# Forget gate first, half of a table on GpSimd, taps moved by sixteen DMAs, film products and low lags spread through the selection

## The chip, the cores and the metric

The kernel runs on one core of a Trainium2 chip, as one program written by hand: each engine has its own list of instructions, and the lists are held together by semaphores alone. PE is the matmul engine (TensorE), DVE the vector engine, ACT the scalar engine, POOL is GpSimd, and SP only issues transfers. The metric is the time in microseconds (us) of one execution on the device, the median of several runs. Lower is better.

## The reference, cut to what matters

A two-layer decoder: x is 2 x 512 rows of 128 numbers, the context 2 x 154 rows of 96, all float32. The first layer is a gated recurrence over a batch of two, a cross-attention with FiLM and an S4D convolution, and attention with experts; the second has two attentions and experts again. The change touches only the first two parts of layer 0:

```python
feat = x @ W_in
V, Q, Fg = jnp.split(feat, 3, axis=-1)
V = gelu(V); Q = gelu(Q); Fg = sigmoid(Fg)
...                                        # a recurrence over the batch axis (2 steps)
x = _layernorm(x + o @ W_out)

scores = einsum('bthd,bghd->bhtg', x @ Wq, ctx @ Wk) / sqrt(32)      # 4 heads, 154 keys
topv, topi = top_k(scores, 32); probs = softmax(topv)
attn_mean = scatter(probs).mean(heads); c_t = attn_mean @ (ctx @ Wv)
y = layernorm(x) * (1 + gate * scale_in(c_t)) + gate * shift_in(c_t)
dtA = exp(log_dt)[:, None] * (A_re + 1j * A_im)                      # 128 channels, 64 states
dC = C * (exp(dtA) - 1) / A
K = 2 * real(einsum('dn,dnl->dl', dC, exp(dtA[:, :, None] * arange(512))))
y = irfft(rfft(y, 1024) * rfft(K, 1024))[:512] + y * D_skip
```

## The kernel before

The 1024 rows are eight tiles (t = 0 to 7) of 128. Everything lies in SBUF; there are eight PSUM banks of 512 columns.

**First stage** (`a_pe`, `a_act`, `a_dve`). PE multiplies the three thirds of `W_in` (values, queries, forget gate, in this order), ACT makes gelu, gelu and sigmoid of them, DVE combines them (`keys`, `qk`, `carried`, `mixed`), PE multiplies `W_out`, DVE adds and normalises in two halves (`norm`, L188 the last step of it; the root is POOL's, L244). Ahead of `keys` DVE computes the table of the convolution (`b_dve_stack`, L419 to L460): eight blocks of 64 columns in `stack`, which PE transposes and ACT copies (`b_act_stack_in`, L528).

**Convolution taps**. The 512 lags are split into 32 low and 16 high ones. `low_r`, `high_r` get angles (ACT, L468 and L475: one instruction for each lag), DVE takes the whole turns off (`b_dve_rounds`: L482 for all 4096 low columns, L484 for the 2048 high ones), POOL subtracts (L494 twice for the low halves, L489 for the high one), ACT takes absolute value and sines (L547, L549, L550, L556) and, later, exponentials (`b_act_low_rates` L534 in two runs of 16 lags, `b_act_high_rates` L541). POOL multiplies: high factors 0 to 3 (L502 twice, L504, L507) and the low factors (L516 twice, by halves of the columns). Then `taps_of_lags` (L735) is 128 small matmuls, one for each channel, 4 to a group of 32 rows of bank 3. ACT copies bank 3 into `taps` by sixteen instructions of 32 rows each, since the row group changes (`b_act_taps`, L566); POOL adds the skip line (L1052), and `taps_spectrum` (L804) transforms `taps`.

**Selection** (`b_dve_attention`). For 16 pairs j of tile and head, DVE finds the 32 largest of 154 scores (`peak` L850, `select` L865 to L877, `selected` L886, `shares` L893, L897). Each pair needs ACT's `exponentials(j)` (L930, L931), which need the peaks, which need the scores (PE L724, copied by `scores_in` L920). PE `gather(t)` (L748, L752) transposes and adds the heads once `diagonals(t)` (L944) are there, ACT copies (`attn_in` L1017, L1018), PE `film_tile(t)` (L790, L791), ACT `film_in(t)` (L952), POOL `modulate(t)` (L1038, L1039), PE `spectrum(t)` (L775). The orders in `b_act_attention`, `b_pool_attention` and `b_pe_attention` are written out by hand, and each engine keeps to its own. After spectrum(7) come DVE products (L1153 on) and the inverse transform on PE (L1092).

Before the selection POOL scales the FiLM weights (`b_pool_pre`, L668 to L672), makes the masks, takes the roots, marks attention columns with a memset (L690), and between the angles and the factors writes the FiLM rows (`b_pool_film_rows`, L654 to L660).

## Time and profile before

| | us |
|---|---|
| median of 3 runs (663.29 to 664.49) | 663.56 |
| the profiled execution | 663.11 |
| its span in the trace | 661.3 |
| PE busy (share of the span) | 603.2 (91%) |
| DVE busy | 439.0 (66%) |
| ACT busy | 287.9 (44%) |
| POOL busy | 246.5 (37%) |

The profiled execution is 0.45 us under the median; 1.8 us of it lie outside the span. The first 130 us hold all that the change touches. The shares of the whole span say little about them: there PE waits longest, and afterwards it is nearly always busy. "Granted clock" is TensorE's clock as a share of full speed: 1.00 and 0.50 are its two levels, 2.4 and 1.2 GHz. Records that overlap in the trace are pipelined.

### The profile page before, as it was taken

What the parts mean: (1) busy time and instruction counts of PE and PEld (TensorE: products, weight loads), DVE (VectorE), ACT (ScalarE), POOL (GpSimd) and SP (SyncE); (2) the same over time, 40 slices, a digit from 0 to 9 for tenths busy, and PEclk for the clock granted to TensorE, in tenths of its full rate; (3) what the DMA queues carried; (4) which work ended last, traced back from release to release, by engine and by line L of the source; (5) the groups of instructions that cost most, each with busy time, mean ns of one, the idle gap of its engine ahead of it and who ended that gap; (6) DMA issues with size and microseconds to landing.
All of it is one profiled execution on the core that took longest, in us unless ns stands there. A gap on an engine that the chain in (4) does not pass through costs nothing.

```text
span 661.3 us, 8811 instructions
## 1 busy us (share of the span) xinstructions
PE 603.2 (91%) x3171; PEld 302.0 (46%) x3172; DVE 439.0 (66%) x1173; ACT 287.9 (44%) x548; POOL 246.5 (37%) x179
## 2 busy tenths in 40 slices
PE   8864959998997999999999998999977999999997
PEld 4432548886572332222222442233622345556566
DVE  6899998556559846766776569668645675333335
ACT  7979968213230554444444333534232334221210
POOL 2899271422531344655465344557334100000001
PEclk9955879999999899999999999999979999999999
DMA  8300006021000000000000000000600000000001
GB/s 321 110 0 0 2 1 256 1 68 60 1 0 1 0 0 1 0 1 1 0 1 0 1 1 0 1 0 1 268 22 1 0 1 0 1 1 0 1 0 33
DMA packets 4945, 19.25 MB, mean 29 GB/s; under 512 B 2053, under 2 KB 3462, under 8 KB 4390
## 3 DMA queue, kind: packets, MB, share of 16 engines
q1 hardware_dynamic: 4902, 18.69, 7.5%
q8 instruction: 25, 0.41, 0.3%
q14 instruction: 18, 0.15, 0.1%
HBM read 18.16 MB, written 0.52 MB: 28 GB/s over the span
## 4 chain that ended last, share of the span: by engine, by line
PE 71%; DVE 14%; ACT 7%; POOL 4%; issue 4%; DMA 0%; POOLq 0%; DVEq 0%; ACTq 0%
PE PS L2401 11%; PE PS L1606 9%; PE PS L1622 8%; PE PS L2422 6%; PE PS L1564 5%; PE PS L1590 3%; PE PS L1692 2%; PE PS L1636 2%; PE PS L1609 2%; DVE SB L1853 2%; DVE SB L199 2%; PE PS L2091 2%; POOL SB L238 2%; ACT SB L468 1%; DVE SB L212 1%
## 5 line engine op out<-in xcount | busy, mean ns | idle before, releaser
L1853 DVE TENSOR_REDUCE SB<-PS 128x2 f32<-128x1024 f32 x64 | 78.4, 1226 | 62.9 <-PE PS L1590 62.8
L1839 POOL TENSOR_TENSOR SB<-SB 128x1024 f32<-128x1024 f32 x32 | 75.2, 2352 | 108.7 <-ACT SB L1791 107.8
L1791 ACT ACTIVATE SB<-PS 128x1024 f32<-128x1024 f32 x64 | 65.6, 1024 | 102.3 <-PE PS L1609 102.2
L2401 PE MATMUL PS<-SB 128*128 128x512 f32 x176 | 78.4, 594 | 0.0
L1606 PE MATMUL PS<-SB 64*128 64x512 f32 x256 | 70.4, 627 | 1.1 <-ACT SB L1795 1.1
L1622 PE MATMUL PS<-SB 128*64 128x512 f32 x256 | 67.6, 610 | 0.5 <-DVE SB L1885 0.5
L238 POOL TENSOR_TENSOR SB<-SB 128x4 f32<-128x4 f32 x18 | 19.3, 1073 | 116.9 <-DVE SB L204 104.3
L2460 ACT ACTIVATE SB<-PS 128x512 f32<-128x512 f32 x44 | 26.2, 597 | 80.2 <-PE PS L2401 78.8
L2486 DVE TENSOR_TENSOR SB<-SB,PS 128x512 f32<-128x512 f32 x44 | 30.0, 688 | 41.8 <-PE PS L2401 40.5
L1876 DVE RECIPROCAL SB<-PS 128x256 f32<-128x256 f32 x32 | 55.6, 1744 | 0.0
L2401 PEld LDWEIGHTS PS<-SB 128*128 128x128 f32 x176 | 32.2, 190 | 35.3 <-issue 33.7
L2466 POOL TENSOR_TENSOR SB<-SB 128x4 f32<-128x4 f32 (+2 forms) x3 | 2.6, 861 | 115.3 <-DVE SB L2510 115.3
L2422 PE MATMUL PS<-SB 128*128 128x128 f32 x320 | 40.0, 280 | 0.0
L1843 POOL TENSOR_TENSOR SB<-SB 128x1024 f32<-128x1024 f32 x16 | 38.2, 2386 | 1.3
L1564 PE MATMUL PS<-SB 128*128 128x512 f32 x64 | 37.4, 667 | 0.7 <-ACT SB L1774 0.7
L2422 PEld LDWEIGHTS PS<-SB 128*128 128x128 f32 x320 | 36.9, 192 | 1.9
L1606 PEld LDWEIGHTS PS<-SB 64*128 64x128 f32 x256 | 20.8, 186 | 29.7 <-issue 13.0
L1622 PEld LDWEIGHTS PS<-SB 128*64 128x64 f32 x256 | 14.3, 135 | 32.7 <-issue 23.8
L1783 ACT ACTIVATE SB<-PS 128x512 bf16<-128x512 f32 x32 | 19.1, 597 | 22.1 <-PE PS L1564 20.9
L2498 DVE SCALAR_TENSOR_TENSOR SB<-PS,SB 128x128 f32<-128x128 f32 x32 | 11.2, 351 | 25.6 <-PE PS L2422 25.5
L1590 PE MATMUL PS<-SB 64*128 64x512 bf16 x128 | 24.7, 382 | 3.2 <-DVE SB L1853 3.2
L869 DVE MAX8 SB<-SB 128x8 f32<-128x154 f32 x96 | 25.6, 308 | 0.0
(415 smaller groups left out, 1125.2 us busy)
## 6 DMA issues: line engine op xcount, KB each, us to landing
SB<-exp SPq DMA_DIRECT2D x1, 4352.0 KB, 14.1
SB<-moe SPq DMA_DIRECT2D x1, 4096.0 KB, 14.5
SB<-dft SPq DMA_DIRECT2D x1, 2304.0 KB, 11.6
SB<-att SPq DMA_DIRECT2D x1, 2048.0 KB, 8.2
SB<-mix SPq DMA_DIRECT2D x1, 768.5 KB, 4.4
SB<-mix SPq DMA_DIRECT2D x1, 640.0 KB, 5.5
SB<-ssm SPq DMA_DIRECT2D x1, 602.0 KB, 6.6
SB<-lat SPq DMA_DIRECT2D x1, 585.0 KB
```

Source lines behind the costliest of these rows:

```text
L238: pool.tensor_tensor(rstd[:, a:z], variance[:, a:z], minus_half[:, a:z], ALU.pow).then_inc(sem("norm_rstd"), 1)
L1564: pe.matmul(bank(b), w[:, 128 * pair:128 * pair + 128], xsT[:, 512 * batch:512 * batch + 512], start=True, stop=True)\
L1590: ins = pe.matmul(bank(4 + h), qb_ring[i % 3][head(h), 128 * qt:128 * qt + 128], kb_ring[i % 3][head(h), :], start=True, stop=True)
L1606: pe.matmul(bank(2 * (n % 2) + h), k_ring[i % 3][head(h), 128 * u:128 * u + 128], q_ring[i % 3][head(h), :], start=True, stop=False)
L1622: ins = pe.matmul(heads_bank(i)[head(h), :], v, expd[i % 2][:, 1024 * kt + 512 * h:1024 * kt + 512 * h + 512], start=(kt == 0), stop=(kt = ...
L1791: act.activation(expd[i % 2][:, 1024 * u:1024 * u + 1024], bank(2 * (u % 2), 2), ACT.Exp).then_inc(sem("d_exp"), 1)
L1839: pool.tensor_tensor(half_sums[half], e[:, 0:1024], e[:, 1024:], ALU.add).then_inc(sem("d_half_sum"), 1)
L1843: pool.tensor_tensor(key_sum, half_sums[0], half_sums[1], ALU.add).then_inc(sem("d_key_sum"), 1)
L1853: dve.tensor_reduce(shift[i % 2][:, qt:qt + DK + 1:DK], two_heads(bank(4, 2)), AX_X, ALU.max, negate=True)\
L1876: ins = dve.reciprocal(unit[:, 256 * k:256 * k + 256], bank(7)[:, 256 * k:256 * k + 256])
L2401: pe.matmul(bank(2 * (i % 3) + side), w, xsT[:, 512 * n:512 * n + 512], start=True, stop=True).then_inc(sem(("top2_w1", "top2_w3")[side]), 1)
L2422: ins = pe.matmul(banks[k][:, 0:128], hidden[q][:, h:h + 128], exp_w["e_w2"][:, at:at + 128], start=False, stop=(c == WHOLE - 1))
```

## The change

1. **First stage**: PE multiplies the forget third first, then queries, then values; ACT makes the sigmoid first. DVE forms `keys` and `carried` as soon as the forget gate is there, `qk` after the queries. The keys and values of the context go to banks 4 and 5, their wait stands before `W_out`, and the score weights (`b_pe_scorer`) follow both halves of `W_out`. The normalisation is unrolled (statistics of half 1 ahead of the last step of half 0).
2. **Table**: DVE keeps the first four blocks of `stack` and the reciprocal. The other seventeen multiplies, adds and three negations are on POOL (`b_pool_stack`). PE transposes two blocks early and two late; DVE copies the first two, ACT the others. DVE makes 8 of the 32 low-lag angles (L470 of the new file), ACT 24.
3. **Rounds by pieces**: low half 0, peak(0), low half 1, peak(1), and the high ones after select(1). The memset of the marked columns moves from POOL to DVE.
4. **POOL's order**: the FiLM weights come after the roots, then both low angles, the marks, the FiLM rows, then the high angles. Low factors go by halves of the lags (strided) with modulate in between; modulate(2) now stands before high factor 3.
5. **ACT's order**: xsT's second half and 14 of the high angles move into the selection; the absolute value stands before exponentials(5), the sines after scores_in(4).
6. **PE's order**: the second half's transposes after score(0), the FiLM products after score(1), spectrum(2) ahead of `taps_of_lags`, spectrum(4) and (5) earlier.
7. **Taps**: one ACT copy into `staged`, then sixteen DMAs of 32 x 128 numbers on SP (`b_sp_taps`), ahead of the transfer of the `moe` weights.

```diff
@@ a_pe
-        for m in range(3):
+        for i in range(2):
+            ins = pe.transpose(bank(7)[:, 128 * i:128 * i + 128], stack[:, 128 * i:128 * i + 128], ident)
+        ins.then_inc(sem("s_stack_turned"), 1)
+        for m in (2, 1, 0):
@@ a_dve
-        dve.wait_ge(sem("a_gates"), 3)
+        dve.wait_ge(sem("a_gates"), 1)
         follow(dve.tensor_scalar(keys, forget, one_less, None, ALU.mult))
+        follow(dve.scalar_tensor_tensor(carried[:, 0:512], keys[:, 512:], 1.0, keys[:, 0:512], ALU.subtract, ALU.mult))
+        dve.wait_ge(sem("a_gates"), 2)
...
+        add(0)
+        spread(0)
+        variances(0)
+        add(1)
+        spread(1)
+        norm_apply(dve, tiled(xsum), tiled(xs), 0).then_inc(sem("stage_half"), 1)
+        variances(1)
+        norm_apply(dve, tiled(xsum), tiled(xs), 1).then_inc(sem("stage_done"), 1)
@@ rounds and angles
-    def b_dve_rounds(dve):
+    def b_dve_low_rounds(dve, h):
+        c = slice(2048 * h, 2048 * h + 2048)
         dve.wait_ge(sem("s_low_products"), 1)
-        dve.tensor_scalar(low_k, low_r, MAGIC, MAGIC, ALU.add, ALU.subtract).then_inc(sem("s_rounds"), 1)
+        dve.tensor_scalar(low_k[:, c], low_r[:, c], MAGIC, MAGIC, ALU.add, ALU.subtract).then_inc(sem("s_rounds"), 1)
+    def b_dve_high_rounds(dve):
         dve.wait_ge(sem("s_high_turns"), 1)
@@ b_pool_high_angles
-        pool.wait_ge(sem("s_rounds"), 2)
+        pool.wait_ge(sem("s_rounds"), 3)
@@ b_pool_low_factor
-        c = slice(2048 * h, 2048 * h + 2048)
-        pool.wait_ge(sem("s_rates"), 1)
-        pool.wait_ge(sem("s_low_waves"), h + 1)
+        lags = slice(LOW // 2 * h, LOW // 2 * h + LOW // 2)
+        pool.wait_ge(sem("s_rates"), h + 1)
+        pool.wait_ge(sem("s_low_waves"), 2)
@@ taps
-        for q in range(a, z):
-            for j in range(4):
-                act.activation(to[32 * q:32 * q + 32, :, :, j], tp[32 * j:32 * j + 32, :, :, q], ACT.Copy)\
-                   .then_inc(sem("s_taps_copied"), 1)
+        act.activation(staged.rearrange("p (q c g) -> p g c q", q=4, c=4), bank(3).rearrange("p (g c q) -> p g c q", c=4, q=4),
+                       ACT.Copy).then_inc(sem("s_taps_copied"), 1)
+    def b_sp_taps(sp):
+        sp.wait_ge(sem("s_taps_copied"), 1)
+        for j in range(4):
+            for q in range(4):
+                sp.dma_start(taps[32 * q:32 * q + 32, 128 * j:128 * j + 128], staged[32 * j:32 * j + 32, 128 * q:128 * q + 128])\
+                  .then_inc(sem("s_taps_copied"), 16)
@@ b_dve_attention
-        b_dve_rounds(dve)
+        b_dve_low_rounds(dve, 0)
         dve.wait_ge(sem("masks_in"), 1)
         peak(0)
+        b_dve_low_rounds(dve, 1)
         peak(1)
+        dve.memset(attn1[96:128, :], 1.0).then_inc(sem("x_clear"), 1)
...
+            if j == 1:
+                b_dve_high_rounds(dve)
@@ b_pool_attention
-        pool.wait_ge(sem("s_taps_copied"), 16)
+        pool.wait_ge(sem("s_taps_copied"), 257)
```

The places on which most rests are these. **POOL**, from the last step of its preparation to the absolute value's input. Before (L668 to L672 are the FiLM weights, L244 the roots, L494 the low and L489 the high angles, L654 to L660 the FiLM rows):

```order
L681 MEMSET SB 1x128 [waits pool_step]
L244 TENSOR_TENSOR SB<-SB 128x4 [waits norm_variance,masks_in]
L244 TENSOR_TENSOR SB<-SB 128x4 [waits norm_variance]
L686 TENSOR_SCALAR SB<-SB 1x128 [waits norm_rstd]
L687 CAST SB<-SB 128x8 [waits pool_step]
L688 TENSOR_SCALAR SB<-SB 128x8 [waits pool_step]
L690 MEMSET SB 32x1024 [waits a_features,pool_step]
L494 TENSOR_TENSOR SB<-SB 128x2048 [waits s_rounds,x_clear]
L489 TENSOR_TENSOR SB<-SB 128x2048 [waits s_rounds]
L494 TENSOR_TENSOR SB<-SB 128x2048 [waits s_rounds]
L654 TENSOR_SCALAR SB<-SB 32x512 [waits s_low_products]
```

And in the change (L238 the roots, L739 to L743 the FiLM weights, L540 the low angles, L714 to L720 the FiLM rows, L535 the high angles):

```order
L238 TENSOR_TENSOR SB<-SB 128x4 [waits norm_variance]
L739 TENSOR_SCALAR SB<-SB 128x512 [waits ssm_in]
L741 TENSOR_TENSOR SB<-SB 128x128 [waits film_w_in]
L742 TENSOR_TENSOR SB<-SB 128x128 [waits pool_step]
L743 TENSOR_TENSOR SB<-SB 128x128
L540 TENSOR_TENSOR SB<-SB 128x2048 [waits s_rounds,film_w_in]
L540 TENSOR_TENSOR SB<-SB 128x2048 [waits s_rounds]
L748 TENSOR_SCALAR SB<-SB 1x128 [waits norm_rstd]
L749 CAST SB<-SB 128x8 [waits pool_step]
L750 TENSOR_SCALAR SB<-SB 128x8 [waits pool_step]
L714 TENSOR_SCALAR SB<-SB 32x512 [waits masks_in]
```

and, without a gap, the rest of the FiLM rows, the high angles and what reads them:

```order
L715 TENSOR_SCALAR SB<-SB 32x2x128 [waits pool_step]
L716 TENSOR_TENSOR SB<-SB 32x128 [waits pool_step]
L717 TENSOR_TENSOR SB<-SB 32x128 [waits pool_step]
L718 TENSOR_TENSOR SB<-SB 32x128 [waits pool_step]
L720 COPY SB<-SB 32x512 [waits pool_step]
L720 COPY SB<-SB 32x512 [waits film_w_in]
L535 TENSOR_TENSOR SB<-SB 128x2048 [waits s_rounds,film_w_in]
L1100 TENSOR_TENSOR SB<-SB 128x8 [waits s_high_turns]
```

The memset is gone; the FiLM weights, a second low half and the FiLM rows now stand ahead of the high angles.

**SP**, the transfer queue, in the change (the line before and the two behind the new ones are as they were, under other numbers):

```order
L1301 DMA SB<-mha 128x1164 [waits film_w_in,x_inputs]
L619 DMA SB<-SB 32x128 [waits s_taps_copied]
L619 DMA SB<-SB 32x128 x15
L1303 DMA SB<-moe 128x8192
L1305 DMA SB<-att 128x4096 [waits s_conv]
```

Sixteen transfers are added, and the `moe` weights go behind them.

**PE** around `taps_of_lags` (L795 in the change; L835 a spectrum, L808 and L812 a gather, L850 and L851 a film tile, L864 the transform of the taps):

```order
L835 MATMUL PS<-SB 128x128 x8
L795 MATMUL PS<-SB 32x16 x128
L808 MATMUL PS<-SB 128x128 x4
L812 MATMUL PS<-SB 32x128 x3
L812 MATMUL PS<-SB 26x128
L835 MATMUL PS<-SB 128x128 x8
L850 MATMUL PS<-SB 128x512
L851 MATMUL PS<-SB 128x512
L864 MATMUL PS<-SB 128x128 x16
```

The first row, spectrum(2), stood behind the second before; what is left between the taps and their transform is one gather, one spectrum and one film tile.

## Rows read from the trace of the kernel before

**Rows 1.** The chain of work that ended last, in time: start us, us, what.

```profile
79.95 9.07 POOL SB L516 x2
89.01 4.47 POOL SB L507
93.61 2.85 PE PS L735 x197
...
...
98.69 3.03 PE PS L775 x16
101.73 0.89 PE PS L748 x8
...
106.67 3.57 PE PS L804 x32
```

**Rows 2.** Timeline, PE: the last gather and the last spectra.

```profile
118.53 1.05 PE L748 MATMUL PS<-SB 128*128 128x128 f32 x8
...
124.00 5.52 PE L775 MATMUL PS<-SB 128*128 128x128 f32 x48
```

**Rows 3.** Timeline, POOL, 24 to 49 us.

```profile
24.14 1.04 POOL L244 TENSOR_TENSOR SB<-SB 128x4 f32<-128x4 f32 x1 [1.00 <-DVE SB L182]
...
29.59 5.45 POOL L494 TENSOR_TENSOR SB<-SB 128x2048 f32<-128x2048 f32 x1
35.00 4.53 POOL L489 TENSOR_TENSOR SB<-SB 128x2048 f32<-128x2048 f32 x1
...
44.12 0.70 POOL L654 TENSOR_SCALAR SB<-SB 32x512 f32<-32x512 f32 x1
...
48.72 0.20 POOL L1030 TENSOR_TENSOR SB<-SB 128x8 f32<-128x8 f32 x1
```

**Rows 4.** Groups of POOL to 125 us: busy us, mean ns, idle before.

```profile
L1063 POOL TENSOR_TENSOR SB<-SB 128x512 f32<-128x512 f32 x1 | 1.3, 1276 | 0.0
L1038 POOL TENSOR_TENSOR SB<-SB 128x128 f32<-128x128 f32 x7 | 2.9, 414 | 17.6 <-ACT SB L952 17.5
```

**Rows 5.** Timeline, DVE and POOL side by side.

```profile
29.43 1.23 DVE L484 TENSOR_SCALAR SB<-SB 128x2048 f32<-128x2048 f32 x1 [0.81 <-ACT SB L475]
141.18 1.08 POOL L1068 TENSOR_TENSOR SB<-SB 128x512 f32<-128x512 f32 x1
141.24 1.87 DVE L212 TENSOR_SCALAR SB<-SB 128x128 f32<-128x128 f32 x4 [1.13 <-POOL SB L238]
162.07 1.12 DVE L212 TENSOR_SCALAR SB<-SB 128x128 f32<-128x128 f32 x4 [1.12 <-POOL SB L238]
```

**Rows 6.** Timeline, ACT, 45 to 85 us.

```profile
45.28 1.90 ACT L547 ACTIVATE SB<-SB 128x2048 f32<-128x2048 f32 x1
...
84.21 0.62 ACT L952 ACTIVATE SB<-PS 128x512 f32<-128x512 f32 x1
```

**Rows 7.** Timeline: ACT's copies of the taps, and SP's issue of small transfers.

```profile
98.73 6.67 ACT L566 ACTIVATE SB<-PS 32x128 f32<-32x128 f32 x16 [3.62 <-PE PS L735]
5.53 0.32 SPq L286 DMA_DIRECT2D SB<-lines  x1
481.62 1.17 SPq L1949 DMA_DIRECT2D SB<-exp  x2
```

**Rows 8.** DMA issues: KB each, median us from issue to landing.

```profile
SB<-exp SPq DMA_DIRECT2D x2, 32.0 KB, 2.1
```

**Rows 9.** Windows of PE: us, length, busy (records), granted clock.

```profile
88.00:89.00 1.00, 0.44 (x9) 1.00 0.00 0
90.00:91.00 1.00, 0.00 (x0) 0.81 0.00 0
...
100.00:101.00 1.00, 1.00 (x7) 0.57 0.51 164
```

**Rows 10.** Timeline, DVE: the selection's longest wait and its last instruction.

```profile
106.15 0.09 DVE L865 MATCH_VALUE_LOAD SB<-SB 128x8 f32 x1 [2.83 <-ACT SB L931]
...
114.79 0.17 DVE L897 RECIPROCAL SB<-SB 128x4 f32<-128x4 f32 x1
```

More of the change, by code:

```diff
@@ L326, in a_pe @@
             ins.then_inc(sem("a_out"), 1)
-            if half == 0:
-                b_pe_scorer(pe)
+        b_pe_scorer(pe)
+        pe.wait_ge(sem("s_stack"), 1)
+        pe.wait_ge(sem("s_stack_in"), 1)
+        for i in (2, 3):
+            ins = pe.transpose(bank(7)[:, 128 * i:128 * i + 128], stack[:, 128 * i:128 * i + 128], ident)
+        ins.then_inc(sem("s_stack_turned"), 1)
     def a_act(act):
@@ L336, in a_act @@
         act.wait_ge(sem("a_features"), 6)
-        act.activation(forget, bank(4, 2), ACT.Sigmoid, scale=-1.0).then_inc(sem("a_gates"), 1)
+        act.activation(gate_v, bank(0, 2), ACT.Gelu).then_inc(sem("a_gates"), 1)
     def a_dve(dve, follow):
@@ new lines, in b_dve_stack, with b_pool_stack @@
+        dve.tensor_copy(stack_T[:, 0:256], bank(7)[:, 0:256]).then_inc(sem("s_stack_in"), 1)
+        dve.wait_ge(sem("s_stack_in"), 1)
+        for l in range(LOW_ACT, LOW):
+            ins = dve.tensor_scalar(lag(low_r, LOW)[:, :, l], turn_T, float(l), ssm["quarter"], ALU.mult, ALU.add)
+        follow(ins)
+    def b_pool_stack(pool, follow):
+        tt = lambda o, a, b, op: pool.tensor_tensor(o, a, b, op)
+        s = stack.rearrange("p (k n) -> p k n", n=N_ST)
+        pool.wait_ge(sem("table_in"), 16)
+        pool.wait_ge(sem("s_trig"), 2)
@@ L665, in b_pool_pre @@
         pool.memset(rest_V, 0.0).then_inc(sem("x_clear"), 1)
+        b_pool_stack(pool, follow)
         pool.wait_ge(sem("small_in"), SMALL)
+        follow(pool.tensor_copy(mask_line, ctx_bytes))
+        follow(pool.tensor_scalar(mask_line, mask_line, 1.0, -NEG, ALU.subtract, ALU.mult))
+        by_batch = mask_line.rearrange("p (b g) -> p b g", b=B)
+        m2 = mask_low.rearrange("p (b h g) -> p b h g", b=B, h=2)
+        for h in range(2):
+            pool.tensor_copy(m2[:, :, h, :], by_batch)
+        pool_rstd_half(pool, 0)
+        pool.tensor_copy(ones_low, ones[0:1, :])
+        pool.memset(zeros_low, 0.0).then_inc(sem("masks_in"), 1)
+        pool_rstd_half(pool, 1)
         pool.wait_ge(sem("ssm_in"), 16)
@@ L805, in taps_spectrum @@
                                     mat[:, 512 * c + 128 * j:512 * c + 128 * j + 128],
-                                    taps[:, 128 * c:128 * c + 128], start=(c == 0), stop=(c == 3))
+                                    taps_of[:, c], start=(c == 0), stop=(c == 3))
             ins.then_inc(sem("s_taps_dft"), 1)
-        for t in range(4):
+        score(0)
+        b_pe_turn(pe, 1)
+        score(1)
+        b_pe_film(pe)
+        for t in (2, 3, 4):
             score(t)
-        score(4)
         gather(0)
@@ L832, in b_pe_attention @@
         gather(6)
+        spectrum(4)
         film_tile(5)
@@ L836, in b_pe_attention @@
         gather(7)
-        spectrum(4)
+        spectrum(5)
         film_tile(7)
-        for t in (5, 6, 7):
+        for t in (6, 7):
             spectrum(t)
@@ L964, in b_act_attention @@
         exponentials(4)
+        b_act_high_sizes(act)
+        exponentials(5)
+        scores_in(4)
         b_act_high_waves(act)
@@ L972, in b_act_attention @@
         exponentials(7)
-        scores_in(4)
         film_in(0)
@@ L1044, in b_pool_attention @@
         modulate(0)
+        b_pool_low_factor(pool, 0)
         modulate(1)
[L1046 removed]
         b_pool_low_factor(pool, 1)
+        modulate(2)
         b_pool_high_factor(pool, follow, 3)
[L1049 removed]
         modulate(3)
[L1051 to L1052 removed]
+        pool.wait_ge(sem("s_taps_copied"), 257)
+        first = taps_of[0:1, 0]
+        pool.tensor_tensor(first, first, skip_line.rearrange("p (j g) -> p j g", j=4), ALU.add).then_inc(sem("s_taps_in"), 1)
         modulate(4)
```

184 lines of the change are left out of this document (92 added, 92 removed).

## The prediction

> **What bounds the kernel now.** I read the chain of waits in time first, since shares of the span say nothing of 130 us in which every engine waits in turn. From 93.61 us it is PE alone: the channel matmuls of the taps (L735) until 98.69, then spectra, gathers and film tiles, the transform of the taps at 106.67, and the last spectrum, whose record ends at 129.5 [rows 1, 2]. So what counts is when PE gets its taps and whether it ever waits behind them. Ahead of 93.61 the chain is POOL: two low factors from 79.95 (9.07 us, waiting for ACT's exponentials) and high factor 3 to 93.5 [rows 1]. ACT itself works through a fixed list from the absolute value at 45.28 to the third film copy at 84.21 [rows 6]; nearly all of it is back to back. The selection on DVE is long, but what ends last is not DVE: it is done at 114.9, and the last gather starts at 118.5 [rows 2, 10]. Its one long wait, 2.83 us, is for ACT, which is then busy with sixteen copies of the taps (6.67 us) [rows 7, 10].
>
> I call S the start of the absolute value on ACT, A the end of high factor 3, T the last channel matmul, X the start of the taps' transform. Now S = 45.3, A = 93.5, T = 98.7, X = 106.7, end of spectra 129.5.
>
> **The first stage.** The forget gate first lets DVE start `keys` when its own table is done. Without the table's second half that is near 10 us, when before it waited for the third of three activations to near 13; and the root of the first stage comes about 1 us before the 25.2 us of now [rows 3] (the rest of the gain goes to PE, whose three pair sums are then late, and to the unrolled halves). On POOL the seventeen moved operations of 64 columns, at most 0.41 us each, the mean of 128 columns [rows 4], fill time in which POOL waited for transfers. I cost all of this at nothing but the 1 us: its cover is that nothing waits for DVE's selection by itself: DVE could be 3.6 us later before the last gather is [rows 2, 10], and more in the change, where X is later. A high round of 1.23 us [rows 5] and the memset go into the selection, and use up what the earlier start gives.
>
> **S, the term I trust least.** ACT is ready for the absolute value at about 45 as before. But it needs the high angles, and these now stand last in POOL's list. Before, POOL had done them at 39.5 (35.00 plus 4.53), with one low angle and the FiLM rows still to come [rows 3]. Now, from the second root at 24.2: FiLM weights 2.6 (1.28 for 512 columns, three of 0.41 [rows 4], and gaps), two low angles 9.1, marks 1.2, FiLM rows 4.6 (44.12 to 48.72), high angles 4.5 [rows 3]. That sums to 46.2. This is the lower bound.
>
> To it comes what DVE does to POOL. Three rows show the engines holding each other up: beside a POOL operation of 1.08 us that had begun 0.06 us before them, four normalising operations of DVE took 1.87 us, elsewhere 1.12; and POOL's first low angle took 5.45 us, the next operation of the same size 4.53, where DVE's high rounds ran beside the first [rows 3, 5]. In the change DVE does its second four normalising operations (1.1 us), two low rounds and a high one (1.23 each) [rows 5] while POOL is in this list without a pause. Each costs POOL its length if it has to wait, nothing if both can go on: 0 to 4.8 us. I take 4.1, near the upper end, since both rows show a wait of nearly the whole overlap. S = 50.3, 5.0 later than now.
> The Trainium skill (SBUF — State Buffer, "SBUF: two separate sides") says that whichever of GpSimd's operation and a two-port or two-input DVE operation starts first holds the shared ports for its whole length, and the other stands still. By it the sum is S = 50.3 as taken, and DVE's rounds may also be held up by up to a whole 4.5 us operation; if ports were shared by bandwidth S would be 46 to 48. The two rows agree with the rule, as far as pairs that short can.
>
> **A.** ACT's list from S to the end of film copy 2 holds the same work as now (exponentials(5) and scores_in(4) only move within it), 38.9 us to that copy's start and 0.6 for it [rows 6]. I add 1.0 for gather(2) and score(6), which PE, idle longer, still does at half clock. So film copy 2 is there at 90.8. New is that modulate(2) (0.9, two of 0.41 [rows 4]) and then high factor 3 (4.5) stand behind it: A = 96.2. The low factors no longer bind: the second gets its exponentials 5 us before that copy and takes 4.5 [rows 1]. Its strided form is not in the trace; between the broadcast high factors and twice the plain one, it is 3.7 to 9 us, and only above 5.5 would it count. A is 2.7 later than now, though S is 5.0 later, since low factor 2 now runs beside ACT's high exponentials. The lower bound from S = 46.2 is 92.1.
>
> **T.** Before, PE stood idle from 88.4, its clock fell after about 2.4 us of that and was back only at 100.9 [rows 9], so the channel matmuls ran at half clock and took 5.1 us with a pause of 1.2 us in them [rows 1]. With spectrum(2) moved into that gap no idle time above 2 us is left, and they run at full clock: 3.9, between 3.1 (all halved but the pause) and 5.1. T = 100.1, which is 1.4 later than now.
>
> **X.** Now 7.9 us lie between T and X, all PE's own work. In the change spectrum(2) is gone from there, and 4.9 are left (101.73 to 106.67 [rows 1]). The taps' way in the change is: one ACT copy 0.6, as film copies of the same size take [rows 6]; SP's start 0.1; sixteen issues; 2.1 from the last issue to its landing [rows 8]; POOL's skip line 0.45; gaps 0.2. A small transfer of 32 rows took SP 0.32, with its gap 0.36, and of 64 rows 0.58 [rows 7]; SBUF to SBUF is not in the trace. Fifteen issues ahead of the last are thus 5.4 to 8.7; I take 5.7, since 32 rows it is. Sum 9.1: X = 109.2, and PE waits 4.2 us. That ACT's copies fall from 6.67 to 0.6 us frees the selection (its 2.83 us wait) but not PE. The range is T plus 8.8 to T plus 12.1. The `moe` weights are issued 6 us later, with 40 us until their use.
>
> **The clock behind X.** 4.2 us without work are more than the 2.4 us after which the clock fell before, and it then took PE 7.3 us from its restart (93.6) to be back [rows 9]. At half clock 7.3 us do the work of 3.65; I take 3.2 lost, 0 if it stays up, 3.65 at most. From X on the same matmuls are left as now, 22.8 us at full clock. The end of spectra is 109.2 + 22.8 + 3.2 = 135.2, against 129.5: 5.7 later. Behind it nothing changes, and PE waits for those spectra before the inverse, so all of it counts. 663.1 + 5.7 = **668.8 us** against the profiled execution; the median of before is 0.45 higher, and I leave that difference in the range.
>
> **Rivals.** (1) *The clock holds* through the 4.2 us: 668.8 - 3.2 = 665.6. For it: the wait is not much longer than 2.4 us. Against: that row.
> (2) *Faster: POOL is not held up and the clock holds.* With S = 46.2, A = 92.1 and X = 105.1, end 127.9, 1.6 earlier: 661.5. The point from which it decides is S = 47.8 with the clock up; with the clock down S would have to be 44.6, below what ACT allows. For it: POOL's waits for DVE are seen for one or two operations only, and the first stage may bring the roots more than 1 us forward. Against: the rows named.
> (3) *The parts cancel*: S near 48 and no loss of clock, or S at 46 with a short one: 662.5 to 664.5.
> (4) *Later still*: SP needs 0.55 for each transfer (X 2.8 later), and DVE's rounds wait for whole POOL operations and POOL for them (S 2 later): 673.6. The selection might then bind too. For it: 0.58 for 64 rows. Against: 0.32 for 32.
> (5) *The change doesn't do what it says*, since ACT, not POOL, sets S: that needs POOL's list of 22 us to fit into 21, rival 2 in effect.
>
> **How the numbers follow.** Forecast 0.50 (own range 666.3 to 671.5, from S 48 to 52.4 and the bounds of T), rival 1 0.17, rivals 2 and 5 0.14, rival 3 0.10, rival 4 0.09. The range 662.0 to 672.5 leaves out half of rival 2 and most of rival 4 and the forecast's tails, 2 in 10. A measurement of this kernel can tell about 0.2% (1.3 us) from no change. Slower by more: the forecast, rival 1 and rival 4 less a few tails, 0.71; within: rival 3 and tails, 0.14; faster: 0.15.
>
> **What would show it.** In the changed profile: the high angles of POOL (L535) end near 50 and the absolute value (L591) starts right behind them; exponentials(6) keep DVE waiting about 2 us near 64; high factor 3 (L553) ends near 96; no half clock at the channel matmuls (L795); one ACT copy of the taps and sixteen issues of about 0.36; PE's longest wait, about 4 us, right ahead of L864, ended by POOL's skip line, and half clock for some 7 us behind it. If L535 ends before 47, or the wait ahead of L864 is under 2 us, the forecast falls; if ACT's list is much shorter than 39 us, too.

## The result and the profile after

The kernel after took 673.88 us (median of four runs, 670.33 to 675.15), beside 663.61 us for the kernel before: ratio 1.0137, 95% interval 1.0101 to 1.0172. Seven further runs on other occasions, six of them against 23 of before, gave 667.98 to 673.96: ratio 1.0094, interval 1.0062 to 1.0127. A ratio is estimated from all runs of both kernels except those more than 1.5% above the fastest run of their kernel, and is not the quotient of the two medians (1.0155 here). The kernel is slower, as forecast. The first median lies above the forecast range, and the profiled run (670.33, span 668.5) inside it, 1.5 us above the forecast. What lies behind each is taken apart below.

The timeline of PE in the kernel after shows the stretch at issue (start us, us, engine line, operation, count, in brackets the idle time ahead and what ended it):

```profile
93.67 1.69 PE L795 MATMUL PS<-SB 128*32 128x16 f32 x181
97.36 0.82 PE L795 MATMUL PS<-SB 128*32 128x16 f32 x75 [1.99 <-issue]
...
103.84 1.02 PE L851 MATMUL PS<-SB 128*128 128x512 f32 x2
111.30 5.97 PE L864 MATMUL PS<-SB 128*128 128x128 f32 x32 [6.44 <-POOL SB L1123]
...
132.82 3.73 PE L835 MATMUL PS<-SB 128*128 128x128 f32 x32
136.74 0.49 PE L1163 MATMUL PS<-SB 128*128 128x128 f32 x2 [0.19 <-DVE SB L1248]
```

A spectrum (L835, from 91.56) now stands ahead of the channel matmuls (L795), and T, the end of their last, is at 98.2, where it was 98.7 [rows 1]. Then PE has 6.7 us of work left and stands still for 6.44 us, until POOL's skip line (L1123) releases the transform of the taps (L864) at X = 111.3, in place of 106.7 [rows 1]. That transform takes 5.97 us, where the same 32 matmuls took 3.73 at full clock in the kernel before. The inverse (L1163) starts at 136.74, where it started at 129.71: 7.0 us later. The profiled runs differ by 7.2 (668.5 against 661.3 us of span). What follows is unchanged: from that point to the first matmul of the last stage it is 403.3 us in this trace and 403.1 in that of before.

What PE waits for is told by the timelines of ACT, SP and POOL, and by the list of DMA issues (KB each, median us from issue to landing):

```profile
98.23 1.07 ACT L611 ACTIVATE SB<-PS 128x512 f32<-128x512 f32 x1 [1.45 <-PE PS L795]
...
99.33 10.10 SPq L619 DMA_DIRECT2D SB<-SB  x16
...
110.71 0.45 POOL L1123 TENSOR_TENSOR SB<-SB 1x128 f32<-1x128 f32 x1 [15.79 <-DMA SB<-SB]
```

```profile
SB<-SB SPq DMA_DIRECT2D x16, 16.0 KB, 1.8
```

The whole way of the taps can be added up: copy 1.07 (to 99.30), sixteen issues in 10.1 us, the last of them begun at 108.8, about 1.9 from there until POOL, released by its landing, starts the skip line (110.7), the skip line 0.45, and X at 111.3. An issue takes 0.59 us (shortest 586 ns, longest 604), 0.63 with the gap to the next. That is the largest piece, and the DMA engines are not what it waits for: they are busy 11% of the time from 100 to 110 us.

Ahead of it POOL's list and ACT show what became of S and A:

```profile
23.23 1.57 POOL L739 TENSOR_SCALAR SB<-SB 128x512 f32<-128x512 f32 x1
24.89 1.51 POOL L741 TENSOR_TENSOR SB<-SB 128x128 f32<-128x128 f32 x1
...
26.89 1.44 POOL L743 TENSOR_TENSOR SB<-SB 128x128 f32<-128x128 f32 x1
28.40 9.05 POOL L540 TENSOR_TENSOR SB<-SB 128x2048 f32<-128x2048 f32 x2
...
38.60 0.70 POOL L714 TENSOR_SCALAR SB<-SB 32x512 f32<-32x512 f32 x1
39.39 1.72 POOL L715 TENSOR_SCALAR SB<-SB 32x256 f32<-32x256 f32 x1
...
44.05 4.51 POOL L535 TENSOR_TENSOR SB<-SB 128x2048 f32<-128x2048 f32 x1
...
83.15 4.67 POOL L563 TENSOR_TENSOR SB<-SB 128x2048 f32<-128x2048 f32 x1 [3.56 <-ACT SB L580]
...
88.98 4.55 POOL L553 TENSOR_TENSOR SB<-SB 128x2048 f32<-128x2048 f32 x1
```

The high angles (L535) end at 48.56, and ACT's absolute value starts at once, S = 48.6. High factor 3 (L553) ends at A = 93.5, where it ended before.

### The profile page after: what moved, and what is told of

Same layout as the page of the kernel before. It is cut to its first block, busy times and chain, and to the rows that moved or that the text cites. A ratio compares the mean times of both kernels' runs of the same rounds, so it can differ in the third digit from the quotient of the medians.

```text
span 668.5 us, 8816 instructions
## 1 busy us (share of the span) xinstructions
PE 601.2 (90%) x3170; PEld 301.4 (45%) x3170; DVE 438.8 (66%) x1164; ACT 279.7 (42%) x525; POOL 251.9 (38%) x198
## 4 chain that ended last, share of the span: by engine, by line
PE 70%; DVE 18%; ACT 6%; issue 3%; POOL 2%; SPq 1%; DMA 0%; POOLq 0%; DVEq 0%; ACTq 0%
PE PS L2472 11%; PE PS L1677 8%; PE PS L1693 8%; PE PS L2493 5%; PE PS L1635 4%; PE PS L1661 3%; PE PS L1707 2%; DVE SB L212 2%; POOL SB L238 2%; DVE SB L199 2%; PE PS L1680 2%; DVE SB L1924 2%; PE PS L2162 2%; PE PS L864 1%; SPq L619 1%
## 5 line engine op out<-in xcount | busy, mean ns | idle before, releaser
L2472 PE MATMUL PS<-SB 128*128 128x512 f32 x176 | 78.4, 594 | 0.0
L238 POOL TENSOR_TENSOR SB<-SB 128x4 f32<-128x4 f32 x20 | 21.3, 1068 | 119.5 <-DVE SB L204 103.6
L2557 DVE TENSOR_TENSOR SB<-SB,PS 128x512 f32<-128x512 f32 x44 | 30.0, 687 | 41.8 <-PE PS L2472 40.5
L1635 PE MATMUL PS<-SB 128*128 128x512 f32 x64 | 36.7, 657 | 0.7 <-ACT SB L1845 0.7
L850 PE MATMUL PS<-SB 128*128 128x512 f32 x16 | 9.5, 679 | 18.7 <-ACT SB L1089 18.1
```

The costliest lines, as they stand in the source:

```text
L238: pool.tensor_tensor(rstd[:, a:z], variance[:, a:z], minus_half[:, a:z], ALU.pow).then_inc(sem("norm_rstd"), 1)
L1635: pe.matmul(bank(b), w[:, 128 * pair:128 * pair + 128], xsT[:, 512 * batch:512 * batch + 512], start=True, stop=True)\
L2472: pe.matmul(bank(2 * (i % 3) + side), w, xsT[:, 512 * n:512 * n + 512], start=True, stop=True).then_inc(sem(("top2_w1", "top2_w3")[side]), 1)
```

## The experiments

**Theory A** was: X is late because of the sixteen transfers, 0.63 us each on one queue, and the copy ahead of them; nearly all of the 7 us is this. **Rivals**: POOL's longer list (S and A late) or the rest of the rearrangement costs it; or the half clock behind the wait is the larger part.

**The taps moved by ACT again.** Only the mover goes back; the channel order and the new layout stay.

```diff
-        act.activation(staged..., bank(3)..., ACT.Copy)          # one copy, then sixteen DMAs on SP
+        for q in range(4):
+            for j in range(4):
+                act.activation(to[32 * q:32 * q + 32, j], tp[32 * j:32 * j + 32, :, :, q], ACT.Copy)
```

> The kernel after, but the taps go to their places by ScalarE's sixteen copies, as in the kernel before, into the new layout; no transfers. Theory A (the sixteen transfers at 0.63 us each set the start X of the taps' transform): X comes about 8 us behind the last channel matmul instead of 13.1, at 106.2, TensorE waits 1.4 us there instead of 6.4, and if the clock then holds another 2.4 us are saved: 663 to 666 us. Theory B (what is late is not the mover but GpSimd's longer list before it, and the rest of the stage): the time stays within 2 us of the kernel after, 670 to 675 us, and the wait on GpSimd ahead of the transform is still 4 us or more.

The profiled run took 661.48 us, nine others 659.96 to 666.55 (median of all 665.42, that of before on this occasion 663.36; ratio to before 1.0007, interval 0.998 to 1.0033). PE, ACT and POOL in its trace:

```profile
97.68 0.82 PE L799 MATMUL PS<-SB 128*32 128x16 f32 x75 [2.19 <-issue]
...
98.55 4.70 ACT L615 ACTIVATE SB<-PS 32x128 f32<-32x128 f32 x16 [1.65 <-PE PS L799]
...
103.33 0.45 POOL L1127 TENSOR_TENSOR SB<-SB 1x128 f32<-1x128 f32 x1 [8.29 <-ACT SB L615]
...
103.93 3.81 PE L868 MATMUL PS<-SB 128*128 128x128 f32 x32 [0.28 <-POOL SB L1127]
...
127.71 1.16 PE L1167 MATMUL PS<-SB 128*128 128x128 f32 x8 [0.19 <-DVE SB L1252]
```

X comes 5.4 us behind T, not 8 as expected, PE waits 0.28 us in place of 6.44, the clock stays full, and the inverse starts at 127.7: 9.0 us before that of the kernel after, and 2.0 before that of the kernel before. Theory A stands, and the rival that puts the cost into the rest of the change falls: without the transfers the rest gains 2 us in this trace. The runs as a whole do not show that gain: the interval of the ratio includes 1. The part on the spread of the runs looks at why single traces and medians differ. A part of the 9.0 us need not be the mover's. In after the clock was also at half from 99 to 102 us, right behind the pause of 1.99 us in the channel matmuls; there it cost nothing, since PE had to wait anyway. In this trace it did not fall there, though the pause was 2.19 us. With the 6.7 us of work that PE had behind T in after, X would have been at 105.2 here, 1.3 us later than it was. The sixteen copies are shorter than I had them: 4.70 us, where the kernel before needed 6.67 [rows 7]. One takes 270 ns (median of sixteen) in place of 394. The operation, its size and its source are the same; what differs is where it writes, 128 adjacent elements per row of the new layout where the old one wrote every fourth. By this sum the new layout shortens the copies by 2.0 us, which is all that the trace gains over before; the old layout was not run with the rest of the change. The change gave the layout to a mover that did not show this gain.

**The other way round: the transfers put into the kernel before.** It is the same mover with its channel order and layout, without anything else of the change.

```diff
-        b_act_taps(act, 0, 4)
+        b_act_taps(act)            # one copy into `staged`
@@ c_sp
-        sp.wait_ge(sem("s_taps"), 1)
+        b_sp_taps(sp)              # sixteen transfers, ahead of the experts' weights
```

> The kernel BEFORE with one part of the change alone: the taps moved by one ScalarE copy and sixteen transfers on SP, with the channel order that goes with them. Theory A (the mover is what costs): the transform of the taps starts 13.1 us behind the last channel matmul instead of 8.0, at 111.8 instead of 106.7, TensorE waits about 5 us, and with the half clock behind that wait the end of the spectra moves by 5 to 7.5 us: 668.5 to 671 us, as slow as the whole change. Theory B (the mover costs only in the company of the rest): under 666 us.

670.32 us (668.68 to 670.89; ratio 1.0083, interval 1.0059 to 1.0107). In its trace:

```profile
98.11 1.04 PE L742 MATMUL PS<-SB 128*32 128x16 f32 x59 [1.40 <-issue]
...
112.25 5.44 PE L811 MATMUL PS<-SB 128*128 128x128 f32 x32 [4.40 <-POOL SB L1060]
...
137.16 1.16 PE L1100 MATMUL PS<-SB 128*128 128x128 f32 x8 [0.19 <-DVE SB L1185]
```

X is 13.1 us behind T (99.15), as in the kernel after, the sixteen issues take 10.09 us, and the inverse starts at 137.16, 7.5 us later than before. So the mover alone costs all that the change costs. Taken away it gives 9, put in alone it takes 7.5. One reason can be read off: here a spectrum still stands behind the channel matmuls, and PE waits 4.40 us where it waited 6.44.

**The clock.** Twenty-four idle matmuls (their result is never read) fill the larger part of PE's wait ahead of the transform: 5.5 us of work, and 3.29 without.

```diff
                 pe.wait_ge(sem("x_scores_in"), NT)
+                stay_warm(pe, 24, 1, ident)
                 pe.wait_ge(sem("s_taps_in"), 1)
```

> The kernel after with 24 idle matmuls on TensorE (their result is never read) ahead of its wait for the taps, so that it does not stand still for 6.4 us there; the wait itself stays. If the half clock behind the wait is the wait's doing, the first transform of the taps takes 3.7 us instead of 6.0 and X stays at 111.3: 2.4 us faster than the profiled run of after, 668 us, and the runs draw together. If the clock falls for what came earlier (the stall in front of the channel matmuls), nothing changes: 670 to 675 us.

The profiled run took 669.38 us, the five others 668.11 to 673.3; the median is 672.5, the ratio to before 1.0134 (interval 1.0099 to 1.0169). On the same occasion the kernel after had a median of 670.28, so the runs as a whole gained nothing, and what follows rests on the traces. Here is PE's granted clock (third number from the end) in two stretches of after, and then one of this kernel:

```profile
106.00:108.00 2.00, 0.00 (x0) 0.00 (x0) 2.00 (x13) 1.00 (x4) 0.00 (x0) 1.00 0.11 25
...
112.00:114.00 2.00, 2.00 (x12) 2.00 (x11) 1.93 (x12) 0.00 (x0) 0.02 (x1) 0.50 0.99 426
```

```profile
112.00:114.00 2.00, 1.48 (x13) 1.48 (x14) 1.95 (x11) 0.00 (x0) 1.22 (x3) 1.00 1.04 360
```

```profile
112.52 3.84 PE L865 MATMUL PS<-SB 128*128 128x128 f32 x32 [3.29 <-POOL SB L1124]
...
135.83 1.16 PE L1164 MATMUL PS<-SB 128*128 128x128 f32 x8 [0.19 <-DVE SB L1249]
```

In after the clock was back at full before the wait, fell inside it (near 109 us) and was at half (1.2 of 2.4 GHz) until near 116. With the idle matmuls it stays up, and the transform takes 3.84 us instead of 5.97: the half clock there is the wait's doing, as far as one trace of each can show. From X to the inverse it is 23.3 us in place of 25.4. But X itself was at 112.5 in this trace, 0.5 of it because T was later, and 0.8 because one of its transfers took 1.35 us to issue. So 2.1 us are the clock's, and of the 7 they are the smaller part. The runs did not draw together and the median did not fall, two points of the expectation that failed.

**POOL's order.** The high angles go ahead of the FiLM rows, which nobody needs before the first film tile.

```diff
-        b_pool_film_rows(pool, follow)
         b_pool_high_angles(pool)
         pool.wait_ge(sem("s_high_turns"), 2)
+        b_pool_film_rows(pool, follow)
```

> The kernel after, with GpSimd's high angles ahead of its film rows instead of behind them (the film rows are wanted only at the first film tile). ScalarE's absolute value then starts 3.6 us earlier or more (the film rows and a copy stood ahead, 4.5 to 5.1 us): 43.5 to 45 instead of 48.6. Theory A (the transfers stand at the end of a chain whose start is ScalarE's list and GpSimd's last factor): GpSimd's last factor and the last channel matmul come 3 to 3.6 us earlier, and the end of the spectra 2 to 3.6 us earlier, 666.5 to 668.5 us for a run like the profiled one. Theory C (TensorE's own list is the limit there, and GpSimd's order costs nothing): within 1 us of after.

Profiled run 666.66 us, median 666.59 (664.44 to 673.51), ratio to before 1.0056, interval 1.0024 to 1.0088.

```profile
44.76 1.91 ACT L591 ACTIVATE SB<-SB 128x2048 f32<-128x2048 f32 x1 [1.39 <-POOL SB L535]
...
45.62 0.86 POOL L715 TENSOR_SCALAR SB<-SB 32x256 f32<-32x256 f32 x1
...
85.22 4.55 POOL L553 TENSOR_TENSOR SB<-SB 128x2048 f32<-128x2048 f32 x1
...
108.12 5.77 PE L864 MATMUL PS<-SB 128*128 128x128 f32 x32 [6.42 <-POOL SB L1123]
...
133.36 1.16 PE L1163 MATMUL PS<-SB 128*128 128x128 f32 x8 [0.19 <-DVE SB L1248]
```

S is 44.8 (3.8 earlier than in after), A 89.8 (3.8 earlier), X 3.2 and the inverse 3.4 earlier. The wait of 6.4 us ahead of the transform is as long as it was. The two losses thus lie one after the other on one chain: high factor 3 moves by what S moves, T by 3.2 (95.0), and the taps' way adds its 13.1 us behind T as before.

**Two queues.** Eight of the transfers are issued by SP and eight by ACT. Is the 0.63 us the issuing engine's, or that of something both share?

```diff
@@ b_sp_taps
-        for j in range(4):
+        for j in range(2):
@@ ACT, behind exponentials(15)
+        for j in (2, 3):
+            for q in range(4):
+                act.dma_start(taps[...], staged[...]).then_inc(sem("s_taps_copied"), 16)
```

> The kernel after, with eight of the sixteen transfers issued on SP and eight on ScalarE, behind its copy of the taps and its next exponentials. If the 0.63 us that one takes on SP are the issuing engine's, two engines issue side by side and X comes 8 x 0.63 = 5 us earlier, at 106.3, or as late as ScalarE gets to them: 2.5 to 5 us less wait on TensorE, 665 to 668 us for a run like the profiled one. If the transfers stand in line behind a common resource, X stays within 1 us of 111.3.

This was the slowest kernel of all: 678.61 us (677.5 to 680.55; ratio to before 1.0219, interval 1.0196 to 1.0242), 8 us above the kernel after's 670.9, the median of its eleven runs. In its trace:

```profile
99.95 5.03 SPq L619 DMA_DIRECT2D SB<-SB  x8
...
102.77 3.82 ACTq L627 DMA_DIRECT2D SB<-SB  x6
...
105.02 0.58 SPq L1312 DMA_DIRECT2D SB<-moe  x1
...
118.38 6.02 PE L872 MATMUL PS<-SB 128*128 128x128 f32 x32 [12.88 <-POOL SB L1132]
```

And of ACT's eight transfers (L627) alone, from issue to landing:

```profile
DMA to landing us min/median/max: 1.8/1.9/11.8
```

The issues did run side by side: all were out at 106.6, 3 us earlier than in after. But SP, done with its half at 105.0, went on to its next instruction, the load of the experts' 4 MB, ahead of ACT's last transfers. One of ACT's took 11.8 us to land, about until the load (12.9 us from its issue at 105.02) was through, and PE waited 12.88 us. In the kernel after all sixteen landed in 1.8 us; there the load stands behind them on the same queue. A wait added to SP tests this:

```diff
         b_sp_taps(sp)
+        sp.wait_ge(sem("s_taps_copied"), 257)
         sp.dma_start(... dram["moe"])
```

> The kernel with eight transfers on SP and eight on ScalarE, and one wait more: SP issues its 4 MB load of the experts' weights only when all sixteen have landed. In the run without that wait the load was issued at 105.0, ahead of ScalarE's last transfers at 106.0, and one of these landed 11.8 us after its issue instead of 1.8. If it was the load that held it up (theory A), X now lies 1.9 us and 0.6 behind the last issue of ScalarE: 109 to 109.5, 2 us earlier than in the kernel after, 668 to 669 us for a run like its profiled one. If two queues hold each other up by themselves (theory B), X stays at 112 or later and the time above 672.

Profiled run 664.52 us, median 665.4 (664.51 to 671.34), ratio to before 1.0034, interval 1.0008 to 1.0059.

```profile
106.89 0.33 SPq L1313 DMA_DIRECT2D SB<-moe  x1
...
107.54 5.44 PE L872 MATMUL PS<-SB 128*128 128x128 f32 x32 [2.99 <-POOL SB L1132]
...
132.44 1.16 PE L1172 MATMUL PS<-SB 128*128 128x128 f32 x8 [0.19 <-DVE SB L1257]
```

```profile
DMA to landing us min/median/max: 1.8/1.8/1.9
```

All of ACT's transfers (last row) now land in 1.8 to 1.9 us, PE waits 2.99 us in place of 6.44, and the inverse starts 4.3 us earlier than in after. I had expected 2 us, having put the last issue where the ungated run had it, 1 us later than here. So the 0.6 us belongs to the engine that issues, and two engines do it side by side; but the small transfers of one queue were held up by the load on the other. The Trainium skill (DMA: Bandwidth & Descriptors, "Issuing engines are not separate DMA queues") says that DMAs of different issuing engines run on the same 16 DMA engines and interleave, and that issuing them from several engines saves only the issuing time, "which is usually small relative to the DMA itself". The traces agree that the issuing time is saved (X 3.8 us earlier) and that what carries the data is shared; how far small transfers get in between a large one they show poorly (11.8 us for one of them). The last clause does not hold for transfers of 16 KB in a row: sixteen issues took 10.1 us, the landing behind the last 1.8.

**The two repairs together**, ACT's copies and the high angles first.

> The kernel after with both repairs: GpSimd's high angles ahead of its film rows, and ScalarE's sixteen copies in place of the transfers. If the two act one after the other on one chain (the channel matmuls wait for GpSimd's last factor, the taps' transform waits for the taps), their gains add up: the last channel matmul at 94.9 as in the run with the high angles first, X 5.5 us behind it at 100.4, the end of the spectra at 124, 3.5 us ahead of the run with ScalarE's copies and 5.7 ahead of the kernel before: 657 to 659 us for a run like the profiled ones, median 657 to 663, faster than the kernel before. If they do not add (TensorE's list ahead of the channel matmuls becomes the bound), it lies at 660 to 661.

Twelve runs: the profiled one 655.05 us, eight at 659.87 to 664.86, two at 665.17 and 668.36, and one at 1184.82; median of all 661.65, ratio to before (of the first nine) 0.9947, interval 0.9921 to 0.9973. That is 0.5% faster than the kernel before, and faster than the kernel after. In the trace of the profiled run the inverse starts at 122.93, 6.8 us before that of the kernel before and 13.8 before that of after: the 9.0 and the 3.4 add up, with 1.4 more, of which 0.9 is there when high factor 3 ends (88.9, where it was 89.8 with the high angles first alone). In a second trace (below) the inverse starts at 123.68. There the clock was at half from 94 to 97 us, behind the pause in the channel matmuls, and PE reached the transform 6.5 us behind T with its own work, where this trace has 5.4.

## Where the runs of one kernel differ

Runs of one kernel lay 7 us apart and more: after 667.98 to 675.15, before mostly 661.5 to 664.8 (68 of 78 runs) but ten at 666.4 to 671.3, the repaired kernel 655.05 to 668.36. Their mean granted clock goes with it (after 0.961 to 0.946). I took a second trace of two kernels to see where.

> The kernel with both repairs once more, for a trace of its usual course: the profiled run took 655.05 us at a mean granted clock of 0.970, the others 659.9 to 662.2 at 0.960. If the 5 us are lost to the clock in one stretch (the theory), this trace has a stretch at half clock that the other has not, and the same order and waits outside it; if they are lost to a wait, the stages are shifted at a full clock.

> The kernel after once more, for a trace of its slower course (673.8 to 675.2 us at a mean granted clock of 0.948 to 0.954; its two traces so far are of runs at 0.957 and 0.959). If the run falls there, the trace shows where the 4 us are: by the theory a stretch at half clock more than in the first profile. If it falls at 668 to 671 it adds nothing but a time.

Both were slower than the first traces: 660.47 and 673.16 us. The table has for each trace the time from the start of the inverse to the first matmul of the last stage, and splits it at the transposes of the context (L1736 in after), which stand near the end of the first of the second layer's two attentions:

| kernel | run | inverse starts | to the last stage | to the split | behind it |
|---|---|---|---|---|---|
| before | 663.1 | 129.7 | 403.1 | 277.6 | 125.5 |
| after | 670.3 | 136.7 | 403.3 | 276.9 | 126.4 |
| after, unchanged, again | 670.9 | 137.6 | 403.0 | 276.6 | 126.4 |
| after, third trace | 673.2 | 136.5 | 406.4 | 277.8 | 128.6 |
| both repairs | 655.1 | 122.9 | 401.8 | 277.0 | 124.8 |
| both repairs, second trace | 660.5 | 123.7 | 406.5 | 278.9 | 127.6 |

The stage that the change touches takes the same within 1.2 us in the traces of one kernel. Of the 4.7 us between the two traces with both repairs (655.1 the quick one, 660.5 the slow one) 1.9 arise in the first attention and 2.8 in the second; of the 3.1 us between the first and the third trace of after 0.9 and 2.2. In the first attention the same wait for DVE stands in both traces with both repairs, and matmuls of L1681 soon behind it take nearly twice as long in the slow one (its two lines are the second pair):

```profile
242.29 0.33 PE L1672 MATMUL PS<-SB 128*128 128x128 f32 x1 [1.32 <-DVE SB L1928]
...
243.73 1.02 PE L1681 MATMUL PS<-SB 64*128 64x512 f32 x4
```

```profile
243.26 0.33 PE L1672 MATMUL PS<-SB 128*128 128x128 f32 x1 [1.33 <-DVE SB L1928]
...
245.02 1.92 PE L1681 MATMUL PS<-SB 64*128 64x512 f32 x4
```

The windows of PE in the second attention, first of the quick trace with both repairs, then of the slow one:

```profile
475.00:480.00 5.00, 3.49 (x8) 1.99 (x9) 2.52 (x9) 1.10 (x2) 0.50 (x1) 0.50 0.28 66
480.00:485.00 5.00, 5.00 (x18) 1.60 (x16) 1.03 (x3) 3.63 (x9) 1.64 (x1) 0.88 0.00 0
...
500.00:505.00 5.00, 2.58 (x17) 1.20 (x17) 2.24 (x2) 0.00 (x0) 0.00 (x0) 1.00 0.00 0
```

```profile
475.00:480.00 5.00, 1.56 (x5) 0.90 (x5) 4.93 (x18) 0.20 (x1) 2.00 (x2) 0.65 0.14 34
480.00:485.00 5.00, 4.37 (x8) 1.83 (x10) 0.77 (x2) 2.11 (x5) 0.00 (x0) 0.50 0.14 31
485.00:490.00 5.00, 5.00 (x18) 1.48 (x14) 1.51 (x6) 3.37 (x6) 1.96 (x2) 0.83 0.00 0
...
505.00:510.00 5.00, 2.59 (x7) 1.14 (x9) 2.24 (x2) 0.00 (x0) 0.00 (x0) 0.72 0.00 0
```

PE has waits of 3.1 and 1.6 us there, for maxima that DVE works out. Behind the first the clock is at half in both traces, for longer in the slow one; behind the second it is so in the slow one alone. Idle matmuls in just these two waits test it, in the repaired kernel and in the unrepaired one:

```diff
+        stay_warm(pe, 12, 0, ident)
         shifts(0)
@@
+        stay_warm(pe, 6, 0, ident)
         shifts(1)
```

> The kernel after, unrepaired, with the same 18 idle matmuls in the same two waits. By the theory its runs, which lay between 668.0 and 675.2, draw together at 667 to 669 us: the real cost of the change in the stage it touches, 7 us by the traces, less what the clock gives back in the late stage. If they stay spread up to 674, the late stage is not where the spread comes from.

> The kernel with both repairs, and 12 and 6 idle matmuls (their result is never read) in TensorE's two waits for the maxima of the second attention, at 474.5 and 501 us, of 3.1 and 1.6 us. Theory: the 5 us between runs of one kernel are lost there; from the end of the spectra to the first matmul of the last stage it took 401.8 us in the quick trace and 406.5 in the slow one, with half clock at 480 to 485 and 505 to 510. Then this stretch takes 401 to 402.5 us in every run, and the runs lie together at 654 to 657 us, 1.0 to 1.4% faster than the kernel before. If the clock falls for other reasons, the runs stay spread from 655 to 662 with a median at 660 to 661.

With the kernel after it came out as expected in the main: nine runs between 667.14 and 670.17, median 669.54 (a tenth took 728.09), ratio to before 1.0077, interval 1.0046 to 1.0107, where eleven without it had lain between 667.98 and 675.15, median 670.9; from the inverse to the last stage it takes 400.5 us in its trace. With the repaired kernel the expectation of 654 to 657 failed: eleven runs at 654.32 to 663.05 and one at 1488.24, median 659.69, ratio to before 0.9915, interval 0.9874 to 0.9956, the lowest median of this study. From the inverse to the last stage its profiled run (658.9 us) takes 403.6 us, not the 401 to 402.5 expected. Yet behind the split of the table it takes 124.4 us, and the unrepaired kernel 124.5, the shortest of all traces: the idle matmuls did their work where they stand. What is lost is lost ahead of them, 279.1 us to the split against 276.0 in the unrepaired kernel, with the clock at half behind the same wait of 1.33 us in the first attention. Half clock also stands behind the channel matmuls, and for a short time behind the filled wait (where the trace of the unrepaired kernel with idle matmuls has some too):

```profile
95.00:100.00 5.00, 5.00 (x69) 4.37 (x58) 4.93 (x29) 4.25 (x16) 0.00 (x0) 0.66 0.84 311
...
480.00:485.00 5.00, 3.87 (x10) 1.98 (x12) 1.73 (x6) 1.83 (x4) 0.00 (x0) 0.67 0.26 59
```

So the late waits carry much of the spread in after, and in the repaired kernel other waits, which no run has filled, carry a spread as large. Why the clock falls in one run and not in another with the same idle times, these runs do not tell. Nor is it shown that 661.65 and 659.69 differ by more than their runs' mixture.

> The kernel after, unchanged, once more on another occasion: its other runs lay at 673.8 to 675.2 us, and only the profiled one at 670.3. If those 4 us are a second course that the same program can take (the theory: another phase of the granted clock in the stretch between 95 and 125 us), single runs come again in two groups some 4 us apart, or the profiled run now shows the late course: a stretch at half clock that the first profile does not have. If they were an accident of that chip, the runs lie together within 1.5 us, as those of the kernel before do. The ratio to the kernel before is 1.011 to 1.017 in the first case.

This last one was the first repetition: its six runs lay between 667.98 and 673.96 without two clean groups, and its profiled run (670.94) repeated the first trace, with a wait of 6.43 us ahead of the transform.

## Why the prediction was right and where it failed

Its direction, its mechanism and the place of it held: PE's longest wait stands ahead of L864, POOL's skip line ends it, the transfers cause it, the clock falls in it, and nothing is given back later. What failed is the size of two terms. The price of an issue, 0.38 us with its gap, measured 0.63, which is 3.8 us for the fifteen ahead of the last. And the loss behind the stage that the change touches was put at nothing, where one trace of after shows 3.1 us more than the first. Without such a loss the median would lie inside the range, as the profiled run does; its three slower runs were not traced. The forecast was 668.8 for a run like the profiled one, which took 670.3. Step by step:

- **The sixteen issues** are the term that failed. I took 5.7 us for fifteen, from one 32-row transfer of 0.32 us [rows 7]; they took 9.5, at 0.63 each. The range of that term reached to 8.7, from the 64-row transfer (0.58), and even that was too short. Both rows were loads from DRAM; none in the trace was from SBUF to SBUF, and I had said so. With rows 7 showing 0.32 and 0.58 for two sizes I chose by the number of rows. In rival 4 I gave the right price, nearly (0.55), a chance of 0.09.
- **The ACT copy** took 1.07 us, not the 0.6 of a film copy of the same size [rows 6]. It writes its rows rearranged, the film copy does not.
- So X was 13.1 behind T, where the sum had 9.1 and its upper bound 12.1.
- **S** was 48.6, not 50.3. The root came 1 us earlier than I had it (22.2 to 23.2), and the engines held each other up by 3.3 us, not 4.1: L739 0.3, L741 1.1, L743 1.0 and L715 0.9 above their undisturbed lengths. L715 takes 0.86 where DVE's high round does not run beside it, and 1.72 where it does. The low angles were not held up at all (9.05 for two). One place shows the turns they take: DVE's high round began at 38.77, inside L714 (38.60 to 39.30), and took 1.63 us (line below) instead of 1.22; L715 began at 39.39, inside that round (to 40.40), and ended 0.7 behind it. The Trainium skill (SBUF — State Buffer, "SBUF: two separate sides") has the shared ports locked by whichever starts first, for its whole length. These rows agree, one after the other, to within 0.2 us: the round was 0.4 longer with 0.5 of L714 left, and L715 0.9 longer with 1.0 of the round left.

```profile
38.77 1.63 DVE L530 TENSOR_SCALAR SB<-SB 128x2048 f32<-128x2048 f32 x1
```

- **A** was 93.5, not 96.2: 1.7 from S, and ACT's list to the end of the film copy took 39.5 us (48.59 to 88.04), not the 40.5 that I had allowed with late scores. The bound by the second low factor did not bind; its strided form took 4.67, near the plain one.
- **T** was 98.2, not 100.1. The channel matmuls ran at full clock as expected; a pause of 1.99 us in them, PE's own issue, was longer than the 1.2 I had.
- **The clock** cost 2.1 us by the trace with idle matmuls, where I had 3.2. It was back about 4.5 us behind X, where I had taken the 7.3 of rows 9.
- **The sum**: T 1.9 early, the taps' way 4.0 late, and from X to the end of the spectra 25.3 us in place of 26.0. That is 1.4 late, 136.6 against 135.2, and the time 1.5 above the forecast. That it was no more is luck: errors of opposite sign, 4.0 us too little for the taps' way against 1.9 too much for T and 0.7 too much behind X.
- **The range** was 662.0 to 672.5. It held six of the eleven runs of after on all occasions, the profiled one among them, but not the first median, since three of those four runs lay 3.4 us and more above the profiled one. None of the three was traced. A run of 673.16 was, and from the inverse to the last stage it took 3.1 us more than the profiled one, 0.9 of them in the first and 2.2 in the second attention, with stretches of half clock in both. I had taken the spread of the kernel before (1.2 us in three runs) for that of the kernel after. More runs of before show 666.4 to 671.3 too. This source of width was in none of my cases, and why it strikes one run and not another stays open.

## What to carry to other kernels

Small transfers in a row cost by their number on the issuing queue: price each by its issue time from the nearest form (source and destination both), and set the sum against what an idle compute engine needs for the same copies; here sixteen copies of 0.29 beat sixteen issues of 0.63. Before splitting such a row over two queues, look at what each queue issues next: a large load issued ahead of the last small ones cost 6.4 us more of wait here than the unsplit row, where the gated split saved 3.5. And where two losses lie on one chain, the one further up (an order on POOL that costs 3.8 us) is worth repairing even if the louder wait is elsewhere. Last, where runs of one kernel spread, take a second trace before pricing a change of a few us, and compare it stage by stage: a single trace of the repaired kernel shows 8.1 us gained, the medians show 2.5.

## What was unexpected of the hardware

- An SBUF-to-SBUF transfer of 32 rows of 512 bytes took SP 0.59 us to issue (a median), ACT 0.61, with 1.8 us to land; a small load of 32 rows from DRAM had taken 0.32.
- A small transfer issued about 1 us behind a load of 4 MB on another queue landed after 11.8 us in the one trace of it, in place of 1.8.
- ACT's copy of 32x128 from PSUM took 270 ns with adjacent elements written and 394 ns with every fourth; the 128x512 copy took 1.07 us with rearranged rows and 0.6 without.
- With the same program and the same idle times in it, the clock fell in some runs and not in others: behind one wait of 1.3 us in the first attention it stayed at full in one trace and fell in another. Between the traces of one kernel this goes with 3.1 to 4.7 us from the inverse to the last stage.
